# Score rows of the late groups: one partition from DRAM, spread by TensorE, copied by ScalarE

## The chip, the cores and the metric

The kernel runs on one core of one Trainium2 chip. The metric is device time in microseconds (us), the median of three runs. A profile of one further execution gives every instruction of the five engines (PE = TensorE, DVE = VectorE, ACT = ScalarE, POOL = GpSimd, SP = SyncE, which here only issues loads), and the DMA engines.

## What is computed

Two layers over 8192 nodes with 128 features; the adjacency matrix `adj` is 8192 x 8192, f32. Layer 0 multiplies `x` by the row-normalised matrix, and by a weight, then adds and normalises. Layer 1 is the part the change is in:

```
x_tangent = logmap0(x, C)
adj_att_par = adj   * sigmoid(s_left[:, None] + s_right[None, :] + b)      # w_par
adj_att_chi = adj.T * sigmoid(s_left[:, None] + s_right[None, :] + b)      # w_chi
support_t = adj_att_chi @ x_tangent + adj_att_par @ x_tangent
x = layernorm(x + proj(expmap0(support_t)))
```

`s_left` and `s_right` are vectors with one score per node. A sigmoid needs a sum of one score per row and one per column for every element of a matrix block.

## The kernel before

**Tiles and units.** Output columns are cut into 8 panels of 1024 nodes (`BP`), rows into 64 tiles of 128. A *unit* is one tile of 128 rows times one panel: 512 units in a fixed order (`plan`). For unit n ACT writes two sigmoids of 128x1024: `chi` into SBUF (L756) and `ps` into a PSUM slot (L773). Each has the panel's *score rows* as input and the tile's column scores as bias. POOL multiplies chi by the block of the matrix (L548), DVE multiplies ps by the transposed block (L1036) and adds both (L1045), and PE takes the sum into the panel's output in PSUM (L1244: two matmuls of 512 columns, each of which shows as two hardware instructions in the profile). Every eighth unit or so is *apart* (`APART`): DVE leaves the sum out, and PE takes both products (L1244 and L1250).

**Score rows.** `scores` has three buffers of [128, 2, 1024]: both rows of a panel (par and chi), the same in all 128 partitions. The rows themselves are written to DRAM (`plcl_d`, L709) as layer 0 finishes a panel. `load_rows` (L715) reads one row of 4 KB and broadcasts it to 128 partitions, 512 KB a load, two loads a panel, on ACT's DMA queue.

**Groups.** Units that stand in a row and belong to one panel are a *group*. Units 0 to 153 are spread between the steps of layer 0. From unit 154 on layer 1 runs alone (the late stage): a group of 64 units for each of the panels 3 to 7, and after each of the first three a group of 8 units that ends one of the panels 0 to 2. Groups thus start at 168, 232, 240, 304, 312, 376, 384 and 448. The eight groups whose rows are loaded anew take turns in score buffers 0 and 1. A buffer's next rows are loaded two units after the buffer's last user (`ROW_LOAD_AT`: units 153, 161, 233, 241, 305, 313, 377, 385), long before they are used.

**What sets the order.** Each engine's program is written out by hand, in a loop over n; semaphores join them. Between the units stand a finished panel's steps, at fixed offsets from a base (`FINALS`: 232, 266, 304, 338, 376, 410, 448, 512): ACT takes the output out of PSUM at +3 (`evacuate`, L796) and squares it at +4 (L807), PE sums the squares at +4 (L1269), ACT takes roots at +7. The output is one PSUM tile, so PE's first product of the next group waits for the evacuation (`out_evac`). For groups of 8 units `evacuate_early_panel` (L801) does the same, four units after the group's end (before unit 243).

**Buffers.** chi has four buffers late on: chi of unit n needs that of unit n - 4, which is free when the sum was made, or, for an apart unit, when PE has read it (`kt_used`). The PSUM slots for ps are two up to unit 194 and three after (`slot_plan`); a slot is free when its unit's sum (or apart product) is made. Loads of the matrix go through a ring of 10 to 11 entries of 1 MB, and SP issues a load as soon as its entry is free.

Of the kernel before, what the change touches and what calls it, by code (L numbers as in the profile page):

```python
# [151 lines left out]

def slot_plan():

    plans = {"unit": {}, "norms": {}, "final": {}}
    holder = {0: ("layer 0", 0), 1: ("passage", 0), 2: None}
    starts = {b + F_NORMS_SLOT: ("norms", k) for k, (_, b) in enumerate(FINALS)}
    starts |= {b + F_SLOT: ("final", k) for k, (_, b) in enumerate(FINALS)}
    uses = []
    for n in range(UNITS):  # L160
        if n in starts:
            uses.append(starts[n] + (n,))
        uses.append(("unit", n, n))
    uses += [("norms", len(FINALS) - 1, UNITS), ("final", len(FINALS) - 1, UNITS)]
    last = 2
    for kind, i, n in uses:
        if n < SLOT_TWO:
            s = 2
        elif n < SLOT_THREE:
            s = 0 if last == 2 else 2  # L170
        else:
            s = (last + 1) % SB
        last = s
        plans[kind][i] = (s, holder[s])
        holder[s] = (kind, i)
    return plans["unit"], plans["norms"], plans["final"]


SLOT_OF_UNIT, SLOT_OF_NORMS, SLOT_OF_FINAL = slot_plan()

# [85 lines left out]
ROW_LOAD_AT = {}  # L268
for _k, (_p, _t, _a) in enumerate(GROUPS):
    if _a == NPAN - 1:  # L270
        ROW_LOAD_AT.setdefault(ROWS_OF[_k][2] + 2, []).append(_k)

# [22 lines left out]
def adj_resnorm_kernel(nc, x_g, xT, g_blk, a_blk, WT, b_row, alpha, w_par, b_par, w_chi, b_chi, out):  # L297
    with ExitStack() as ctx:
# [21 lines left out]
        prcr = sb("prcr", [P, UPP * 2])  # L320
        ones = sb("ones", [P, 1])
        ident = sb("ident", [P, P])
        WTs = sb("WTs", [P, D])

        w4 = sb("w4", [P, 4])
# [62 lines left out]

        const_in = sem("const_in")
        ident_ready = sem("ident_ready")  # L390
        oma_ready = sem("oma_ready")
        bpc2_ready = sem("bpc2_ready")
        x_in = [sem(f"x_in{G}") for G in range(NG)]
# [28 lines left out]
        rowp_ready = sem("rowp_ready")  # L422
        rows_ready = sem("rows_ready")
        rows_out = sem("rows_out")

        c_ready = sem("c_ready")
        p_ready = sem("p_ready")
# [28 lines left out]
        def slot_free(eng, before):  # L456

            kind, i = before
            if kind == "unit" and i in APART:
                eng.wait_ge(m1_ready, i + 1)  # L460
            elif kind == "unit":
                eng.wait_ge(k_ready, SUMS[i])
            elif kind == "norms":
                eng.wait_ge(f_norm, i + 1)
            elif kind == "final":
                eng.wait_ge(v_ready, i + 1)
            elif kind == "layer 0":
                eng.wait_ge(y_evac, NPAN)
            else:
                eng.wait_ge(rows_ready, NPAN)  # L470
                eng.wait_ge(prcr_ready, NPAN)
# [58 lines left out]
        @block.gpsimd  # L530
        def _(pool):
            pool.memset(ones[:, :], 1.0).then_inc(ident_ready, 1)
            pool.memset(epsc[:, :], LN_EPS).then_inc(ident_ready, 1)
            pool.memset(ident[:, :], 0.0).then_inc(ident_ready, 1)
            pool.wait_ge(ident_ready, 3)
# [112 lines left out]
        def _(act):  # L648
# [63 lines left out]
            def load_rows(p, b):  # L712
                act.wait_ge(rows_out, 32 * (p + 1))
                for k in range(2):
                    act.dma_start(scores[:, b, k, :], plcl_d[k:k + 1, p * BP:(p + 1) * BP].to_broadcast([P, BP])) \  # L715
                        .then_inc(l_in[b], 16)

            def passage(r, tick):
                if tick == T_LOADX and r + 1 < NPAN:
                    load_xT(r + 1)  # L720
                if tick == T_SCALEX and r + 1 < NPAN:
                    scale_xT(r + 1)
                if tick == T_STD:
                    deviation(r)
                if tick == T_X1:
                    normalise(r)
                if tick == T_SQ:
                    squares(r)
                if tick == T_NRM:
                    norms(r)  # L730
                if tick == T_LN:
                    logarithm(r)
                if tick == T_XT:
                    tangent(r)
                if tick == T_XTT:
                    copy_turned_tangent(r)
                if tick == T_COPY:
                    copy_rows(r)
                if tick == T_LOADL and r < EARLY:
                    load_rows(r, r)  # L740


            def sigmoids(n):
                k, p, jt = UNIT[n]
                row, c, _ = rows_of(n)
                act.wait_ge(l_in[row], 32 * c)
                act.wait_ge(prcr_ready, jt // TPP + 1)
                b, before = buffer_of(n, CB)
                if before in APART:
                    act.wait_ge(kt_used, before + 1)  # L750
                elif before is not None:
                    act.wait_ge(k_ready, SUMS[before])
                elif b == CB:
                    act.wait_ge(l0_used, PAIRS)
                    act.wait_ge(res_ready, NPAN)
                act.activation(chi(n), scores[:, row, 1, :], ACT.Sigmoid,  # L756
                               bias=prcr[:, 2 * jt + 1:2 * jt + 2]).then_inc(c_ready, 1)
                if n in OWN_AT:
                    i = OWN_AT[n]
                    if i >= 2:  # L760
                        act.wait_ge(m1_ready, OWN[i - 2] + 1)
                    elif i == 1:
                        act.wait_ge(l0_used, PAIRS)
                        act.wait_ge(res_ready, NPAN)
                    else:
                        act.wait_ge(acc_added, ADDED_ALL)
                    dst = own_par[i % 2]
                else:
                    s, before = SLOT_OF_UNIT[n]
                    if before is not None:  # L770
                        slot_free(act, before)
                    dst = slots[s]
                act.activation(dst, scores[:, row, 0, :], ACT.Sigmoid,  # L773
                               bias=prcr[:, 2 * jt:2 * jt + 1]).then_inc(p_ready, 1)

            def next_rows(k):
                b, _, e = ROWS_OF[k]
                act.wait_ge(c_ready, e + 1)
                act.wait_ge(p_ready, e + 1)
                load_rows(GROUPS[k][0], b)  # L780

            def take_out(k):
                p, _, a = GROUPS[k]
# [104 lines left out]
            for n in range(N_EARLY, UNITS):  # L888
# [7 lines left out]
                    take_out(EVAC_AT_UNIT[n])  # L896
                if n - F_EVAC - 1 in LAST_OF_EARLY:
                    evacuate_early_panel(LAST_OF_EARLY[n - F_EVAC - 1])
                sigmoids(n)
            k = NPAN - 1  # L900
            act.preload_act_table(ACT.Sqrt)
# [256 lines left out]
        def _(pe):  # L1158
# [105 lines left out]
            def norms(k):  # L1264
# [4 lines left out]
                    ins = pe.matmul(slots[s][:, j:j + 1], columns(sqT, j), ones[:, 0:1], start=True, stop=True)  # L1269
                ins.then_inc(norms_ready, 1)  # L1270

            def turn(k):
                p, b = FINALS[k]
                pe.wait_ge(out_evac, GROUP_OF_FINAL[k] + 1)
# [20 lines left out]
            for n in range(N_EARLY, UNITS):  # L1295
                passage(NPAN - 1, LATE_PE.get(n - LATE0))
                for k, (_, b) in enumerate(FINALS):
                    if n == b + F_NORMS:
                        norms(k)
                    if n == b + F_TURN:  # L1300
                        turn(k)
                if n + 2 in OWN_AT:
                    turn_own(n + 2)
                products(n)
            norms(NPAN - 1)
            turn(NPAN - 1)
# [30 lines left out]
```

## Time and profile before

| | |
|---|---|
| median of 3 runs | 2198.63 us (2198.61 to 2199.72) |
| the profiled execution | 2200.13 us, span of its instructions 2198.3 us |
| busy, whole span | PE 2006.2, DVE 1929.8, POOL 1340.4, ACT 1318.0 us |
| DMA | 820.37 MB, mean 373 GB/s |
| score row loads | 22 of 512 KB, median 10.4 us from issue to landing |

A row of the timeline gives start, length, engine, line, operation, names and, in brackets, how long the engine stood idle before it and what ended that. Matmul ends are modelled; start to start is the safer reading. DMA share is the mean busy share of the 16 DMA engines. Times are from the first instruction of the profiled execution.

### The profile page before, as it was taken

How to read it: one execution, taken by the hardware profiler on the slowest of the kernel's cores; microseconds unless marked ns; L12 is line 12 of the kernel's file. 1: busy time of each engine (PE TensorE's matmuls, PEld its weight loads, DVE VectorE, ACT ScalarE, POOL GpSimd, SP SyncE). 2: the span in 40 equal slices, each digit the busy share in tenths (PEclk: the TensorE clock that was granted, in tenths of full speed). 3: DMA queues.
4: the chain of work that ended last, by engine and by line, in shares of the span. 5: the costliest groups of instructions: out<-in, count | busy, mean ns of one | idle time of the engine just before them, and what ended most of it. 6: DMA issues, size and time to landing. Idle time of an engine off the chain costs nothing. (4 is left out here: it accounts for less than half of the span.)

```text
span 2198.3 us, 18369 instructions
## 1 busy us (share of the span) xinstructions
PE 2006.2 (91%) x5072; PEld 898.4 (41%) x5072; DVE 1929.8 (88%) x1864; ACT 1318.0 (60%) x1508; POOL 1340.4 (61%) x639
## 2 busy tenths in 40 slices
PE   7999999999999998999999978898888888889886
PEld 3444444444444444444444433343333333334333
DVE  5757787988989989898999989999998998989896
ACT  0001324454464454454453588988989988989996
POOL 0000304534455554644544677999998998999996
PEclk9999999999999999999999988999999999999998
DMA  9978988989989989988989998999999999999993
GB/s 338 362 273 291 400 288 349 406 343 384 388 329 409 414 331 363 392 337 337 416 345 348 422 408 329 421 420 421 422 410 421 421 419 394 421 421 398 398 393 143
DMA packets 128453, 820.37 MB, mean 373 GB/s; under 512 B 14880, under 2 KB 27488, under 8 KB 31328
## 3 DMA queue, kind: packets, MB, share of 16 engines
q1 hardware_dynamic: 113392, 799.06, 90.7%
q10 hardware_dynamic: 14960, 20.13, 2.7%
q8 instruction: 42, 0.69, 0.1%
q14 instruction: 59, 0.48, 0.1%
HBM read 814.88 MB, written 4.26 MB: 373 GB/s over the span
## 5 line engine op out<-in xcount | busy, mean ns | idle before, releaser
L548 POOL TENSOR_TENSOR chi<-chi,ring 128x1024 f32<-128x1024 f32 x326 | 834.4, 2573 | 628.5 <-ACT chi L756 572.4
L1244 PE MATMUL ps<-keys,xtA 128*128 128x512 f32 x2048 | 981.3, 611 | 140.1 <-DVE keys L1045 110.5
L1171 PE MATMUL ps<-ring,xA 128*128 128x512 f32 x2048 | 918.4, 598 | 33.8 <-DMA xA<-in_x_g 15.2
L773 ACT ACTIVATE ps<-scores,prcr 128x1024 f32<-128x1024 f32 x492 | 544.2, 1106 | 394.2 <-DVE keys L1045 377.5
L1244 PEld LDWEIGHTS ps<-keys,xtA 128*128 128x128 f32 x2048 | 377.6, 193 | 683.8 <-issue 653.0
L935 DVE TENSOR_TENSOR dsum<-dsum,ring 128x2048 f32<-128x2048 f32 x240 | 594.1, 2475 | 30.4 <-DMA ring<-in_g_blk 24.4
L1171 PEld LDWEIGHTS ps<-ring,xA 128*128 128x128 f32 x2048 | 387.5, 192 | 519.1 <-issue 493.9
L1045 DVE TENSOR_TENSOR keys<-ps,chi 128x1024 f32<-128x1024 f32 x426 | 521.6, 1225 | 85.6 <-issue 31.3
L756 ACT ACTIVATE chi<-scores,prcr 128x1024 f32<-128x1024 f32 x426 | 483.8, 1136 | 16.3 <-DMA scores<-plcl_d 8.5
L1036 DVE TENSOR_TENSOR ps<-ps,ring 128x1024 f32<-128x1024 f32 x348 | 425.5, 1223 | 44.4 <-ACT ps L773 39.0
L548 POOL TENSOR_TENSOR chi<-chi,xA 128x1024 f32<-128x1024 f32 x79 | 185.7, 2366 | 18.4 <-ACT chi L756 18.4
L548 POOL TENSOR_TENSOR xA<-xA,ring 128x1024 f32<-128x1024 f32 x54 | 127.8, 2366 | 14.3 <-ACT xA L756 14.3
L756 ACT ACTIVATE xA<-scores,prcr 128x1024 f32<-128x1024 f32 x86 | 98.0, 1139 | 42.2 <-PE ps L1250 42.1
L1036 DVE TENSOR_TENSOR ps<-ps,xA 128x1024 f32<-128x1024 f32 x90 | 110.0, 1222 | 9.6 <-ACT ps L773 9.6
L541 POOL TENSOR_TENSOR dsum<-dsum 128x1024 f32<-128x1024 f32 x8 | 18.8, 2353 | 127.9 <-DVE dsum L935 125.4
L1250 PE MATMUL ps<-xA,xtA 128*128 128x512 f32 x148 | 70.5, 599 | 0.0
L1045 DVE TENSOR_TENSOR keys<-ps,xA 128x1024 f32<-128x1024 f32 x49 | 60.0, 1225 | 2.7 <-POOL xA L548 1.0
L548 POOL TENSOR_TENSOR xA<-xA 128x1024 f32<-128x1024 f32 x23 | 54.3, 2362 | 4.1 <-ACT xA L756 4.1
L756 ACT ACT_TABLE_LOAD x28 | 35.9, 1283 | 34.4 <-DVE prcr L1002 27.9
L557 POOL TENSOR_TENSOR acc<-taken,acc 128x1024 f32<-128x1024 f32 x15 | 37.3, 2487 | 31.0 <-ACT taken L789 31.0
L548 POOL TENSOR_TENSOR chi<-chi,scores 128x1024 f32<-128x1024 f32 x21 | 49.5, 2363 | 6.2 <-ACT chi L756 6.2
L661 ACT ACT_TABLE_LOAD x1 | 1.3, 1283 | 76.5 <-issue 76.5
(122 smaller groups left out, 820.9 us busy)
## 6 DMA issues: line engine op xcount, KB each, us to landing
ring<-in_g_blk SPq DMA_DIRECT2D x443, 1024.0 KB, 8.6
ring<-in_a_cols SPq DMA_DIRECT2D x190, 1024.0 KB, 10.0
xA<-in_a_cols SPq DMA_DIRECT2D x51, 1024.0 KB, 11.9
xA<-in_g_blk SPq DMA_DIRECT2D x44, 1024.0 KB, 10.0
scores<-in_a_cols SPq DMA_DIRECT2D x15, 1024.0 KB, 11.7
scores<-in_g_blk SPq DMA_DIRECT2D x15, 1024.0 KB, 10.7
scores<-plcl_d ACTq DMA_DIRECT2D x22, 512.0 KB, 10.4
xA<-in_x_g ACTq DMA_DIRECT2D x64, 64.0 KB, 11.8
```

The costliest lines, as they stand in the source:

```text
L541: pool.tensor_tensor(out=dsum[:, 0:BP], in0=dsum[:, 0:BP], in1=dsum[:, BP:2 * BP], op=ALU.add).then_inc(folded, 1)
L548: pool.tensor_tensor(out=chi(n), in0=chi(n), in1=half(t, n), op=ALU.mult).then_inc(m2_ready, 1)
L557: pool.tensor_tensor(out=at, in0=taken[:, :], in1=at, op=ALU.add).then_inc(acc_added, 1)
L661: act.activation(yb[:, :], yb[:, :], ACT.Copy, scale=oma[:, 0:1]).then_inc(xTs_scaled, 1)
L756: act.activation(chi(n), scores[:, row, 1, :], ACT.Sigmoid, bias=prcr[:, 2 * jt + 1:2 * jt + 2]).then_inc(c_ready, 1)
L773: act.activation(dst, scores[:, row, 0, :], ACT.Sigmoid, bias=prcr[:, 2 * jt:2 * jt + 1]).then_inc(p_ready, 1)
L935: dve.tensor_tensor(out=dsum[:, :], in0=dsum[:, :], in1=t, op=ALU.add).then_inc(deg_added, 1)
L1036: dve.tensor_tensor(out=keys(n) if n in APART else s, in0=s, in1=other, op=ALU.mult).then_inc(m1_ready, 1)
L1045: dve.tensor_tensor(out=keys(n), in0=slots[SLOT_OF_UNIT[n][0]], in1=chi(n), op=ALU.add).then_inc(k_ready, 1)
L1171: ins = pe.matmul(Y[:, h * BANK:(h + 1) * BANK], xA[:, tile * D:(tile + 1) * D], t[:, tt * BP + h * BANK:tt * BP + (h + 1) * BANK], start= ...
L1244: ins = pe.matmul(outp[:, h * BANK:(h + 1) * BANK], xtA[:, jt * D:(jt + 1) * D], keys(n)[:, h * BANK:(h + 1) * BANK], start=begins, stop=i ...
L1250: ins = pe.matmul(outp[:, h * BANK:(h + 1) * BANK], xtA[:, jt * D:(jt + 1) * D], chi(n)[:, h * BANK:(h + 1) * BANK], start=False, stop=is_ ...
```

## The change

For the eight late groups the load brings each row to one partition only: `scores[0:1, b, k, :]`, 4 KB. It is issued one unit earlier, one unit after the buffer's last user. PE then multiplies a row of ones [1, 128] with it (`send_rows`: two matmuls of 512 columns into a PSUM slot), which gives the row in all 128 partitions, and ACT copies it to `scores` (`copy_sent_rows`). `slot_plan` gives each row a turn in the rotation of the PSUM slots, as if it were a unit. The sends stand on PE before the products of the units `CAST_AT` - 2, the copies on ACT before the sigmoids of `CAST_AT` + 1; `CAST_AT` is 156, 157, 164, 165, 236, 237, 244, 245, 308, 309, 316, 317, 380, 381, 388 and 389. The three early panels keep their broadcasts. The core of the diff:

```
-        ROW_LOAD_AT.setdefault(ROWS_OF[_k][2] + 2, []).append(_k)
+        ROW_LOAD_AT.setdefault(ROWS_OF[_k][2] + 1, []).append(_k)
+ROW_CAST = 4
+CAST_LAG = 1
+CASTS = [(_k, _s) for _n in sorted(ROW_LOAD_AT) for _k in ROW_LOAD_AT[_n] for _s in range(2)]
+    _n = ROWS_OF[_k][2] + 1 + ROW_CAST + _s
...
+        if n in CAST_AT:
+            uses.append(("rows", CAST_AT[n], n))
         uses.append(("unit", n, n))
...
+            def load_late_rows(p, b):
+                act.wait_ge(rows_out, 32 * (p + 1))
+                for k in range(2):
+                    act.dma_start(scores[0:1, b, k, :], plcl_d[k:k + 1, p * BP:(p + 1) * BP]).then_inc(l_in[b], 16)
+            def copy_sent_rows(i):
+                k, which = CASTS[i]
+                act.wait_ge(rows_sent, i + 1)
+                act.activation(scores[:, ROWS_OF[k][0], which, :], slots[SLOT_OF_ROWS[i][0]], ACT.Copy).then_inc(rows_here, 1)
...
                 act.wait_ge(c_ready, e + 1)
                 act.wait_ge(p_ready, e + 1)
-                load_rows(GROUPS[k][0], b)
+                load_late_rows(GROUPS[k][0], b)
...
+                if n - CAST_LAG in CAST_AT:
+                    copy_sent_rows(CAST_AT[n - CAST_LAG])
                 sigmoids(n)
...
+            def send_rows(i):
+                pe.wait_ge(l_in[b], 32 * c)
+                s, before = SLOT_OF_ROWS[i]
+                slot_free(pe, before)
+                for h in range(BP // BANK):
+                    ins = pe.matmul(slots[s][:, at], ones_row[:, :], scores[0:1, b, which, at], start=True, stop=True)
+                ins.then_inc(rows_sent, 1)
...
+                if n + 2 in CAST_AT:
+                    send_rows(CAST_AT[n + 2])
                 products(n)
```

PE from the start of group 232, before (products of a unit are x2, an apart unit has L1250 too; L1236 loads the panel's earlier sum, L1269 sums the squares):

```order
L1236 MATMUL ps<-acc,ident 128x512 x2
L1244 MATMUL ps<-keys,xtA 128x512 x6
L1250 MATMUL ps<-xA,xtA 128x512 x2
L1244 MATMUL ps<-keys,xtA 128x512 x2
L1269 MATMUL ps<-ones,dsum 128x1 x8
L1244 MATMUL ps<-keys,xtA 128x512 x14
L1250 MATMUL ps<-xA,xtA 128x512 x2
```

The same place in the changed kernel (L1277, L1285, L1291 and L1310 are those lines, L1322 is the send):

```order
L1277 MATMUL ps<-acc,ident 128x512 x2
L1285 MATMUL ps<-keys,xtA 128x512 x4
L1322 MATMUL ps<-scores,ones_row 128x512 x2
L1285 MATMUL ps<-keys,xtA 128x512 x2
L1291 MATMUL ps<-xA,xtA 128x512 x2
L1322 MATMUL ps<-scores,ones_row 128x512 x2
L1285 MATMUL ps<-keys,xtA 128x512 x2
L1310 MATMUL ps<-ones,dsum 128x1 x8
L1285 MATMUL ps<-keys,xtA 128x512 x12
L1322 MATMUL ps<-scores,ones_row 128x512 x2
L1285 MATMUL ps<-keys,xtA 128x512 x2
L1291 MATMUL ps<-xA,xtA 128x512 x2
```

Two sends now stand around the apart unit 234 and the next two around the apart unit 242.

ACT at unit 235, before (L796 takes the panel out, L807 squares it):

```order
L796 ACTIVATE dsum<-ps 128x1024
L756 ACTIVATE chi<-scores,prcr 128x1024
L773 ACTIVATE ps<-scores,prcr 128x1024
L807 ACTIVATE dsum<-dsum 128x1024
L756 ACTIVATE chi<-scores,prcr 128x1024
L773 ACTIVATE ps<-scores,prcr 128x1024
L756 ACTIVATE chi<-scores,prcr 128x1024
L773 ACTIVATE ps<-scores,prcr 128x1024
L756 ACTIVATE xA<-scores,prcr 128x1024
```

The same place in the changed kernel (L835, L795, L812 and L846 are those lines, L752 is the copy):

```order
L835 ACTIVATE dsum<-ps 128x1024
L795 ACTIVATE chi<-scores,prcr 128x1024
L812 ACTIVATE ps<-scores,prcr 128x1024
L846 ACTIVATE dsum<-dsum 128x1024
L795 ACTIVATE chi<-scores,prcr 128x1024
L812 ACTIVATE ps<-scores,prcr 128x1024
L752 ACTIVATE scores<-ps 128x1024
L795 ACTIVATE chi<-scores,prcr 128x1024
L812 ACTIVATE ps<-scores,prcr 128x1024
L752 ACTIVATE scores<-ps 128x1024
L795 ACTIVATE xA<-scores,prcr 128x1024
```

A copy now stands ahead of the sigmoids of unit 237 and another ahead of those of unit 238 (the chi that goes to xA).

## Rows read from the trace of the kernel before

**Rows 1.** Windows: busy us PE, PEld, DVE, ACT, POOL; granted clock, DMA share, GB/s.

```profile
1400.00:1500.00 100.00, 89.25 (x233) 38.91 (x232) 91.53 (x79) 91.51 (x89) 95.53 (x47) 1.00 1.01 421
...
1859.00:1867.00 8.00, 7.49 (x14) 3.28 (x15) 6.63 (x7) 7.17 (x9) 7.75 (x9) 0.79 1.02 422
```

**Rows 2.** Waits, 1300 to 2180 us: who for whom, total us, times, longest.

```profile
ACT xA L756 <- PE ps L1250: 42.1, 27, 2.4
POOL chi L548 <- ACT chi L756: 38.7, 24, 6.3
...
POOL xA L548 <- ACT xA L756: 19.9, 17, 5.4
```

**Rows 3.** Waits of SP's load queue in the same stretch.

```profile
SPq L519 <- POOL chi L548: 609.3, 160, 8.0
```

**Rows 4.** Groups by line: busy us, mean ns of one, idle before.

```profile
L789 ACT ACTIVATE taken<-ps 128x1024 f32<-128x1024 f32 x15 | 15.2, 1013 | 17.3 <-PE ps L1244 17.2
```

**Rows 5.** The tile plcl_d: its DMAs, ns to issue min/median/max, us to landing.

```profile
L709 ACTq DMA_DIRECT2D plcl_d<-yb x16: 246/290/521, 213.8 to 1368.7; - x16
...
DMA to landing us min/median/max: 5.2/10.4/16.3
```

**Rows 6.** Timeline of PE from group 232 on.

```profile
1468.27 5.31 PE L1244 MATMUL ps<-keys,xtA 128*128 128x512 f32 x12
1473.42 1.88 PE L1250 MATMUL ps<-xA,xtA 128*128 128x512 f32 x4
1475.14 1.88 PE L1244 MATMUL ps<-keys,xtA 128*128 128x512 f32 x4
...
1489.76 5.42 PE L1244 MATMUL ps<-keys,xtA 128*128 128x512 f32 x12 [2.31 <-ACT acc L801]
1495.02 1.88 PE L1250 MATMUL ps<-xA,xtA 128*128 128x512 f32 x4
```

**Rows 7.** Timeline of ACT at the same place (evacuation, units 235, 237, 238; 243, 246).

```profile
1465.37 1.02 ACT L796 ACTIVATE dsum<-ps 128x1024 f32<-128x1024 f32 x1 [0.98 <-PE ps L1244]
1466.29 1.14 ACT L756 ACTIVATE chi<-scores,prcr 128x1024 f32<-128x1024 f32 x1
...
1471.40 1.14 ACT L756 ACTIVATE chi<-scores,prcr 128x1024 f32<-128x1024 f32 x1
...
1475.42 1.15 ACT L756 ACTIVATE xA<-scores,prcr 128x1024 f32<-128x1024 f32 x1 [1.88 <-PE ps L1250]
...
1488.70 1.00 ACT L801 ACTIVATE acc<-ps 128x1024 f32<-128x1024 f32 x1
...
1497.02 1.15 ACT L756 ACTIVATE xA<-scores,prcr 128x1024 f32<-128x1024 f32 x1 [1.01 <-PE ps L1250]
```

**Rows 8.** Timeline of POOL there: units 238, 239 and 246.

```profile
1476.71 2.35 POOL L548 TENSOR_TENSOR xA<-xA 128x1024 f32<-128x1024 f32 x1 [1.43 <-ACT xA L756]
1481.67 2.37 POOL L548 TENSOR_TENSOR chi<-chi,xA 128x1024 f32<-128x1024 f32 x1 [2.60 <-ACT chi L756]
...
1499.19 2.37 POOL L548 TENSOR_TENSOR xA<-xA,ring 128x1024 f32<-128x1024 f32 x1
```

**Rows 9.** Timeline of ACT at groups 304 and 376: units 310, 318, 382, 390.

```profile
1659.95 1.15 ACT L756 ACTIVATE xA<-scores,prcr 128x1024 f32<-128x1024 f32 x1 [1.88 <-PE ps L1250]
...
1681.64 1.15 ACT L756 ACTIVATE xA<-scores,prcr 128x1024 f32<-128x1024 f32 x1 [0.59 <-PE ps L1250]
...
1845.07 1.15 ACT L756 ACTIVATE xA<-scores,prcr 128x1024 f32<-128x1024 f32 x1 [1.88 <-PE ps L1250]
...
1868.46 1.15 ACT L756 ACTIVATE xA<-scores,prcr 128x1024 f32<-128x1024 f32 x1 [2.29 <-PE ps L1250]
```

**Rows 10.** Timeline of PE after the second evacuation at group 376.

```profile
1859.51 7.11 PE L1244 MATMUL ps<-keys,xtA 128*128 128x512 f32 x12 [2.31 <-ACT acc L801]
```

**Rows 11.** Timeline of DVE: the sum of unit 156, the product of unit 158.

```profile
1253.47 1.23 DVE L1045 TENSOR_TENSOR keys<-ps,chi 128x1024 f32<-128x1024 f32 x1 [2.27 <-POOL chi L548]
...
1257.01 1.22 DVE L1036 TENSOR_TENSOR ps<-ps,ring 128x1024 f32<-128x1024 f32 x1
```

More of the change, by code:

```diff
@@ L153, in slot_plan @@
 def slot_plan():
-    plans = {"unit": {}, "norms": {}, "final": {}}
+    plans = {"unit": {}, "norms": {}, "final": {}, "rows": {}}
     holder = {0: ("layer 0", 0), 1: ("passage", 0), 2: None}
@@ L175, in slot_plan @@
         holder[s] = (kind, i)
-    return plans["unit"], plans["norms"], plans["final"]
-SLOT_OF_UNIT, SLOT_OF_NORMS, SLOT_OF_FINAL = slot_plan()
+    return plans["unit"], plans["norms"], plans["final"], plans["rows"]
 ROWS_GONE = max(k for k, (p, _, a) in enumerate(GROUPS) if p == 2 and a < NPAN - 1)
@@ L270 @@
     if _a == NPAN - 1:
-        ROW_LOAD_AT.setdefault(ROWS_OF[_k][2] + 2, []).append(_k)
+        ROW_LOAD_AT.setdefault(ROWS_OF[_k][2] + 1, []).append(_k)
+ROW_CAST = 4
+CAST_LAG = 1
+CASTS = [(_k, _s) for _n in sorted(ROW_LOAD_AT) for _k in ROW_LOAD_AT[_n] for _s in range(2)]
+CAST_AT = {}
+for _i, (_k, _s) in enumerate(CASTS):
+    _n = ROWS_OF[_k][2] + 1 + ROW_CAST + _s
+    assert _n not in CAST_AT
+    CAST_AT[_n] = _i
+CAST_OF = {_k: 2 * _i + 2 for _i, (_k, _) in enumerate(CASTS[::2])}
+SLOT_OF_UNIT, SLOT_OF_NORMS, SLOT_OF_FINAL, SLOT_OF_ROWS = slot_plan()
 MORE = LATE0 + 16
@@ L322, in adj_resnorm_kernel @@
         ident = sb("ident", [P, P])
+        ones_row = sb("ones_row", [1, P])
         WTs = sb("WTs", [P, D])
@@ L390, in adj_resnorm_kernel @@
         ident_ready = sem("ident_ready")
+        ones_row_ready = sem("ones_row_ready")
         oma_ready = sem("oma_ready")
@@ L424, in adj_resnorm_kernel @@
         rows_out = sem("rows_out")
+        rows_sent = sem("rows_sent")
+        rows_here = sem("rows_here")
         c_ready = sem("c_ready")
@@ L466, in slot_free @@
                 eng.wait_ge(v_ready, i + 1)
+            elif kind == "rows":
+                eng.wait_ge(rows_here, i + 1)
             elif kind == "layer 0":
@@ L532, in _ @@
             pool.memset(ones[:, :], 1.0).then_inc(ident_ready, 1)
+            pool.memset(ones_row[:, :], 1.0).then_inc(ones_row_ready, 1)
             pool.memset(epsc[:, :], LN_EPS).then_inc(ident_ready, 1)
@@ L745, in sigmoids @@
                 row, c, _ = rows_of(n)
-                act.wait_ge(l_in[row], 32 * c)
+                if k in CAST_OF:
+                    act.wait_ge(rows_here, CAST_OF[k])
+                else:
+                    act.wait_ge(l_in[row], 32 * c)
                 act.wait_ge(prcr_ready, jt // TPP + 1)
@@ L1270, in norms @@
                 ins.then_inc(norms_ready, 1)
+            def send_rows(i):
+                k, which = CASTS[i]
+                b, c, _ = ROWS_OF[k]
+                pe.wait_ge(l_in[b], 32 * c)
+                pe.wait_ge(ones_row_ready, 1)
+                s, before = SLOT_OF_ROWS[i]
+                slot_free(pe, before)
+                for h in range(BP // BANK):
+                    at = slice(h * BANK, (h + 1) * BANK)
+                    ins = pe.matmul(slots[s][:, at], ones_row[:, :], scores[0:1, b, which, at], start=True, stop=True)
+                ins.then_inc(rows_sent, 1)
             def turn(k):
```

## The prediction

> **What bounds the kernel now.** The changed work lies in the late stage, from unit 154 on (about 1240 us to 2175 us). I read that stage in three steps. First the windows [rows 1]: in 100 us DVE is busy 91.53, ACT 91.51, POOL 95.53 and PE 89.25 us, and the DMA engines are full (share 1.01, 421 GB/s). Five resources are near their ends at once, so shares do not decide; the waits must. Second, who waits for whom between 1300 and 2180 us [rows 2]: POOL waits 38.7 + 19.9 = 58.6 us for ACT's sigmoids, ACT 42.1 us for PE's L1250, and no row of that answer names a DMA. SP instead waits 609.3 us in that stretch for POOL to free ring entries [rows 3]: data wait for compute, not compute for data. So compute sets the pace and the full DMA engines are a closed loop's queue.
>
> Third, the places where POOL stops. At a change of groups (first unit 232, then 304 and 376) ACT must take the finished panel out before PE may begin the next group. PE begins late and works off a backlog: after the evacuation at 1465.37 [rows 7] it runs 12, 4 and 4 instructions without a gap [rows 6]. ACT's chi for unit 238 needs the buffer of unit 234, an "apart" unit whose last reader is PE's L1250, and waits 1.88 us for it [rows 7]. POOL then stands 1.43 us before unit 238 and 2.60 us before unit 239 [rows 8]. Eight units later PE waits 2.31 us for the next evacuation [rows 6] and ACT waits 1.01 us before unit 246 [rows 7]. Near these places PE's backlog, then ACT, is the critical path. The change puts its new work exactly there, two units after each place's start.
>
> **What is removed.** 16 of the 22 broadcast loads of 512 KB go; 16 loads of one 4 KB row come. 16 x 524,288 B = 8.39 MB; at 421 GB/s [rows 1] that is 19.9 us of DMA time. I cost it at nothing gained, because no engine waits for a load in that stage [rows 2]; ring entries only land earlier and lie longer.
>
> The Trainium skill, "DMA: Bandwidth & Descriptors" (Specifications), puts the fabric's ceiling at 435 GB/s, so 421 would be 97% of what can be had and 19.3 us of it would come free. The trace agrees that the engines are full; by that rule alone the kernel would gain, and that is the second rival below.
>
> **What is added, on its own.** PE: 16 sends of two 128x512 f32 matmuls, four hardware instructions each. No row shows a matmul from one partition. The nearest is L1244 with the same 512 columns: 12 take 5.31 us, four take 1.72 (1473.42 to 1475.14 [rows 6]). Bounds: 0.43 us (if one partition cost as little as one of the four instructions) and 3.4 us (the same four at the halved clock, seen as 0.79 mean with 12 in 7.11 us [rows 1, 10]). I take 1.72, the row of equal shape. ACT: 16 copies PSUM to SBUF of 128x1024; L789 is that instruction, 1013 ns [rows 4], and 0.92 us start to start (1465.37 to 1466.29, [rows 7]). So 27.5 us of PE and 14.7 us of ACT in all; POOL's added memset lies before the first load and costs nothing visible.
>
> The Trainium skill, "TensorE: Matmul & The Clock Gate" (Step-by-step: what each phase is for), says a matmul's time goes by its columns and that "row count K doesn't matter here" for the weight load. By it a send from one partition costs as much as from 128, which is the value taken; no run here shows it yet.
>
> **What it does at a group change, worked at unit 232.** (1) The first pair of sends stands on PE before the products of units 234 and 235. Unit 234's L1250 therefore ends 1.72 us later, and the second send another 1.72 us after that. ACT's second copy stands before the sigmoids of unit 238, waits for the second send, and takes 0.92 us: chi 238 starts 1.72 + 1.72 + 0.92 = 4.4 us after its present 1475.42. The first copy disappears in the wait of 1.88 us that was there. Queued behind the waiting copy are all later sigmoids, since ACT runs in order; POOL was already idle for 1.43 and 2.60 us there [rows 8], so it cannot absorb it: +4.4 us on POOL. (2) The row load of the next group moves from unit 241 to 240 and now waits for the sigmoid that ACT has just started. The issue of two loads (0.29 us each by the small store of L709, [rows 5]) is no longer covered: c 240 starts about 0.7 us later, half of which POOL feels: +0.4 us. (3) The second pair stands before the products of units 242 and 243, again in a backlog that starts at an evacuation (1488.70, [rows 7]). chi 246 comes 4.4 us later for the same reason. POOL's product 246 started at 1499.19, while its input was ready at 1497.02 + 1.15 = 1498.17; less 0.15 us of signal, 0.9 us of that is slack: +3.5 us, and the ACT part of (2), 0.3 us, comes in here. Sum: 4.4 + 0.4 + 3.5 + 0.3 = 8.6 us. After that POOL and DVE run back to back again, so nothing is given back.
>
> At units 304 and 376 the same 1.88 us stand before the fourth-later chi, and 0.59 and 2.29 us in place of 1.01 [rows 9]. I take 8.6 us for each. In the last, PE had its clock halved for a moment (12 in 7.11 us, [rows 10]); if it is not halved there now, 1.7 us come back.
>
> **The first two late groups** (units 154 to 166) differ: only two PSUM slots turn over, and a row takes one of them for two units. Unit 157's sigmoid into PSUM must wait for unit 156's sum, which ends at 1253.47 + 1.23 = 1254.70 [rows 11]; then come that sigmoid, the copy (0.92) and unit 158's two sigmoids (at most 1.15 each, [rows 7]): DVE can take unit 158 at 1254.70 + 0.92 + 3 x 1.15 = 1259.1 at the latest, not 1257.01: +2.1 us, and 1.9 with the sigmoids' overlap of about 0.1. The second pair falls on DVE's residual work of the last passage, which covers it; I allow 0.6 us. Together 2.5 us, between 0 and 6.
>
> **Sum.** 3 x 8.6 + 2.5 = 28.3 us. The profiled execution took 2200.13 us (span 2198.3) and would take 2228.4; the median of the runs is 2198.63, 1.5 lower, so **2227 us**.
>
> **Rivals.** About 0.2% (4.4 us) is what a measurement of this kernel can tell from no change.
> (A) Only ACT's own time counts. If PE sends in gaps before its backlog, ACT pays 16 x 0.92 = 14.7 us and nothing waits: 2213. For: ACT runs 91% busy [rows 1]. Against: the order of PE puts the sends behind two products of the new group, and those behind the evacuation.
> (B) Faster: loads bind after all. Place: the ring in the late stage. If units followed landings, 19.9 us would go: 2198.6 - 19.9 = 2179. For: DMA share 1.01. Against: [rows 2, 3]. It decides from the point where POOL or DVE waits for a ring entry; here neither does.
> (C) Hidden: the copies fit into ACT's present waits (1.88 and 1.01 us, each over 0.92) and the sends into PE's 2.31 us: 2199 to 2203. Against: those waits exist because PE is late, and the sends make it later.
> (D) More: the small rows land late. A broadcast needs 5.2 to 16.3 us, median 10.4 [rows 5]; from the issue for the second pair to its first send I count about 11 us. If a 4 KB row behind a full ring takes 16, PE waits 5 us more at three places; or the clock halves during the sends. Either gives 10 to 15 us more: 2240.
>
> **Chances.** Forecast 0.50, (A) 0.20, (D) 0.13, (C) 0.10, (B) 0.07. Faster 0.07, within 0.2% 0.10, slower 0.83. The range takes in the forecast, (A) with the first groups' low bound and one-instruction sends (2207), and (D) with its upper end (2242).
>
> **What would show it.** Right: the sends' rows at 1.7 us for four; ACT rows of the copy with waits of 0.5 to 3 us released by PE; POOL's stops before units 238 and 239 grown by about 4.4 us together and a new stop before 246; DMA share below 1.0 in the late stage. Wrong: sends much shorter than 1.7 us; POOL's waits for ACT not above 58.6 us by some 25 us; any wait of PE for the rows' landing (then D); a load wait that vanished (then B).

## The result and the profile after

| | before | changed kernel |
|---|---|---|
| median of 4 runs each, same chip | 2198.62 us (2198.38 to 2199.72) | 2229.68 us (2227.95 to 2232.71) |
| the profiled execution | 2200.13 us, span 2198.3 us | 2227.95 us, span 2226.2 us |
| DMA, whole span | 820.37 MB | 812.04 MB |

The ratio is 1.0137, with a 95% interval of 1.0124 to 1.0150: the changed kernel is about 30 us slower. The forecast was 2227 us. The profiled execution was the fastest of the four, with a mean granted clock of TensorE of 0.984 (the slowest, 2232.71 us, had 0.979), so the traces show 27.8 of the 31 us between the medians; the rest lies in executions that have no trace.

**Where the time came from.** For each unit I subtract its start in the trace of before from its start in the trace of after; I take DVE's product (L1036 before, L1077 after) where nothing else is said. A number that stays the same over many units means that nothing is lost there. The difference is 0.99 us at unit 154, where the late stage begins. It grows at three places and is constant between them:

| place | before it | after it | grows by |
|---|---|---|---|
| units 154 to 194 (first two late groups) | 0.99 | 0.98 | 0.0 |
| units 236 to 250 (group 232) | 1.01 | 10.69 | 9.7 |
| units 303 to 350 (group 304) | 10.75 | 20.00 | 9.3 |
| units 375 to 430 (group 376) | 20.02 | 28.85 | 8.8 |
| units 430 to 510 | 28.85 | 28.80 | 0.0 |

Inside the first place: from unit 236 to 238 it grows from 1.01 to 5.90 (first pair of rows, 4.9), at unit 240 to 6.15 (row loads, 0.25), and from unit 244 to 250 from 6.31 to 10.69 (second pair, 4.4).

The timeline of PE after, at group 232 (start, length, engine, line, operation, names, shapes, count, and in brackets the idle time before and what ended it). L1322 is the send; this answers [rows 6]:

```profile
1467.51 1.98 PE L1277 MATMUL ps<-acc,ident 128*128 128x512 f32 x4 [1.11 <-ACT dsum L835]
1469.33 3.60 PE L1285 MATMUL ps<-keys,xtA 128*128 128x512 f32 x8
1472.85 1.98 PE L1322 MATMUL ps<-scores,ones_row 1*128 1x512 f32 x4
1474.76 1.98 PE L1285 MATMUL ps<-keys,xtA 128*128 128x512 f32 x4
1476.58 1.88 PE L1291 MATMUL ps<-xA,xtA 128*128 128x512 f32 x4
1478.39 1.98 PE L1322 MATMUL ps<-scores,ones_row 1*128 1x512 f32 x4
...
1496.47 3.70 PE L1285 MATMUL ps<-keys,xtA 128*128 128x512 f32 x8 [3.12 <-ACT acc L840]
1500.10 1.98 PE L1322 MATMUL ps<-scores,ones_row 1*128 1x512 f32 x4
```

The sends stand inside PE's backlog: from 1467.51 on PE has no gap. A send takes 1472.85 to 1474.76, that is 1.91 us, where the products of before took 1.72 [rows 6].

The timeline of ACT after, at the same place. L752 is the copy, L795 the chi sigmoid, L747 the load of two rows; this answers [rows 7]:

```profile
1466.43 1.02 ACT L835 ACTIVATE dsum<-ps 128x1024 f32<-128x1024 f32 x1 [0.99 <-PE ps L1285]
...
1474.87 1.03 ACT L752 ACTIVATE scores<-ps 128x1024 f32<-128x1024 f32 x1 [2.35 <-PE ps L1322]
1475.79 1.14 ACT L795 ACTIVATE chi<-scores,prcr 128x1024 f32<-128x1024 f32 x1
...
1480.41 1.03 ACT L752 ACTIVATE scores<-ps 128x1024 f32<-128x1024 f32 x1 [2.47 <-PE ps L1322]
1481.33 1.14 ACT L795 ACTIVATE xA<-scores,prcr 128x1024 f32<-128x1024 f32 x1
...
1488.51 0.53 ACTq L747 DMA_DIRECT2D scores<-plcl_d  x2
...
1502.11 1.03 ACT L752 ACTIVATE scores<-ps 128x1024 f32<-128x1024 f32 x1 [1.48 <-PE ps L1322]
...
1507.65 1.03 ACT L752 ACTIVATE scores<-ps 128x1024 f32<-128x1024 f32 x1 [2.47 <-PE ps L1322]
1508.58 1.14 ACT L795 ACTIVATE xA<-scores,prcr 128x1024 f32<-128x1024 f32 x1
```

Each copy waits 1.5 to 2.5 us for its send, and the sigmoid behind it starts 0.92 us after the copy does. The chi of unit 238 (1481.33) no longer waits for its apart buffer, as it did for 1.88 us before [rows 7]: the copy ahead of it waits longer.

The timeline of POOL after, units 237 to 239 and then 245 and 246; this answers [rows 8]:

```profile
1477.07 2.35 POOL L573 TENSOR_TENSOR chi<-chi,ring 128x1024 f32<-128x1024 f32 x1 [3.05 <-ACT chi L795]
1482.61 2.36 POOL L573 TENSOR_TENSOR xA<-xA 128x1024 f32<-128x1024 f32 x1 [3.19 <-ACT xA L795]
1487.57 2.36 POOL L573 TENSOR_TENSOR chi<-chi,xA 128x1024 f32<-128x1024 f32 x1 [2.60 <-ACT chi L795]
...
1504.32 2.35 POOL L573 TENSOR_TENSOR chi<-chi,ring 128x1024 f32<-128x1024 f32 x1 [1.11 <-ACT chi L795]
1509.85 2.37 POOL L573 TENSOR_TENSOR xA<-xA,ring 128x1024 f32<-128x1024 f32 x1 [3.19 <-ACT xA L795]
```

POOL stands 3.05 + 3.19 + 2.60 = 8.84 us before units 237 to 239, where it stood 1.43 + 2.60 = 4.03 us [rows 8]: 4.8 us more, the size of the first pair. Before units 245 and 246 it now stands 4.30 us. Who waits for whom after, from 1300 to 2208 us (total us, times, longest), to be held against [rows 2]:

```profile
POOL chi L573 <- ACT chi L795: 51.3, 33, 6.3
...
POOL xA L573 <- ACT xA L795: 33.0, 18, 5.4
ACT xA L795 <- PE ps L1291: 29.8, 19, 2.4
ACT scores L752 <- PE ps L1322: 25.5, 12, 2.5
```

POOL waits 84.3 us for ACT's sigmoids, 25.7 us more than before. ACT waits 25.5 us for sends, all of it in the twelve copies of the three places. No row names a DMA. Windows after (start and end, length, busy us of PE, PEld, DVE, ACT, POOL, then the granted clock, DMA share, GB/s):

```profile
1400.00:1500.00 100.00, 87.77 (x228) 37.49 (x226) 87.32 (x75) 88.67 (x87) 90.51 (x41) 1.00 0.98 404
```

Against [rows 1] the DMA share fell from 1.01 to 0.98, and POOL's busy time from 95.53 to 90.51 us: the same work is spread over more time.

### The profile page after: what moved, and what is told of

The parts are those of the page before. It is cut to its first block and busy times, and to the rows that moved or that the text cites. A ratio compares the mean times of both kernels' runs of the same rounds, so it can differ in the third digit from the quotient of the medians.

```text
span 2226.2 us, 18530 instructions
## 1 busy us (share of the span) xinstructions
PE 2031.4 (91%) x5136; PEld 903.2 (41%) x5136; DVE 1930.7 (87%) x1864; ACT 1332.9 (60%) x1524; POOL 1341.4 (60%) x640
## 2 busy tenths in 40 slices
DMA packets 126181, 812.04 MB, mean 365 GB/s; under 512 B 14640, under 2 KB 27248, under 8 KB 29056
## 5 line engine op out<-in xcount | busy, mean ns | idle before, releaser
L1285 PE MATMUL ps<-keys,xtA 128*128 128x512 f32 x2048 | 977.8, 608 | 142.9 <-DVE keys L1086 111.2
L812 ACT ACTIVATE ps<-scores,prcr 128x1024 f32<-128x1024 f32 x492 | 544.2, 1106 | 386.9 <-DVE keys L1086 369.4
L1285 PEld LDWEIGHTS ps<-keys,xtA 128*128 128x128 f32 x2048 | 373.5, 192 | 688.1 <-issue 654.1
L795 ACT ACTIVATE chi<-scores,prcr 128x1024 f32<-128x1024 f32 x426 | 484.0, 1136 | 20.8 <-DMA scores<-plcl_d 7.7
L1077 DVE TENSOR_TENSOR ps<-ps,ring 128x1024 f32<-128x1024 f32 x348 | 425.7, 1223 | 65.0 <-ACT ps L812 62.7
L1077 DVE TENSOR_TENSOR ps<-ps,xA 128x1024 f32<-128x1024 f32 x90 | 110.0, 1222 | 15.9 <-ACT ps L812 15.9
L795 ACT ACTIVATE xA<-scores,prcr 128x1024 f32<-128x1024 f32 x86 | 97.9, 1139 | 29.8 <-PE ps L1291 29.8
L566 POOL TENSOR_TENSOR dsum<-dsum 128x1024 f32<-128x1024 f32 x8 | 18.8, 2354 | 128.4 <-DVE dsum L976 126.0
L1291 PE MATMUL ps<-xA,xtA 128*128 128x512 f32 x148 | 69.5, 592 | 0.0
```

Source lines behind the costliest of these rows:

```text
L566: pool.tensor_tensor(out=dsum[:, 0:BP], in0=dsum[:, 0:BP], in1=dsum[:, BP:2 * BP], op=ALU.add).then_inc(folded, 1)
L795: act.activation(chi(n), scores[:, row, 1, :], ACT.Sigmoid, bias=prcr[:, 2 * jt + 1:2 * jt + 2]).then_inc(c_ready, 1)
L812: act.activation(dst, scores[:, row, 0, :], ACT.Sigmoid, bias=prcr[:, 2 * jt:2 * jt + 1]).then_inc(p_ready, 1)
L1077: dve.tensor_tensor(out=keys(n) if n in APART else s, in0=s, in1=other, op=ALU.mult).then_inc(m1_ready, 1)
L1285: ins = pe.matmul(outp[:, h * BANK:(h + 1) * BANK], xtA[:, jt * D:(jt + 1) * D], keys(n)[:, h * BANK:(h + 1) * BANK], start=begins, stop=i ...
L1291: ins = pe.matmul(outp[:, h * BANK:(h + 1) * BANK], xtA[:, jt * D:(jt + 1) * D], chi(n)[:, h * BANK:(h + 1) * BANK], start=False, stop=is_ ...
```

## The experiments

The times of the kernel before that go with each ratio were taken on the same chip as the experiment: medians 2200.22 us (the first four experiments) and 2198.85 us (the last three).

**Rows only.** Do the loads bind? This takes the kernel before and makes the late loads small, without sends or copies: 127 partitions keep the scores that stood there, here as in the copies and the sends alone below.

```
-                load_rows(GROUPS[k][0], b)
+                load_late_rows(GROUPS[k][0], b)
```

> The kernel before, with the late groups' rows loaded to one partition only, nothing sent and nothing copied: the spreading over partitions is left out, so the late sigmoids use old rows. This is the removed DMA work alone, 8.39 MB less. Theory (no engine waits for a load in the late stage, compute sets the pace): within 0.2% of before, 2196 to 2202 us; DMA share in the late windows falls from 1.01 to about 0.98 and nothing else moves. Rival (loads bind, 19.9 us of DMA time come free): about 2179 us.

Measured: 2198.45 us, ratio 0.9994 (0.9985 to 1.0002). In its trace, which was longer in layer 0, the difference to before is 6.2 us at unit 154 and 7.0 us at unit 510, without a place where it falls. So 8.39 MB less at a share of 1.01 buys nothing: the loads bind nothing, and the rival with 2179 us falls. The expected share of about 0.98 came in two of the five windows of 100 us from 1400 to 1900 us only (0.98 and 0.97, against 1.01 and 0.99 before); the other three stayed at 1.01.

**Second pairs later.** Is the second pair dear because it stands in the backlog behind an evacuation? Its sends and copies are moved 18 units on (42 for the first group), where PE has gaps.

```
+LATER = {19: 42, 21: 18, 23: 18, 25: 18}
...
-    _n = ROWS_OF[_k][2] + 1 + ROW_CAST + _s
+    _n = ROWS_OF[_k][2] + 1 + ROW_CAST + LATER.get(_k, 0) + _s
```

> The changed kernel with the second pair of each place (rows of the groups of 8 units' successors in buffer 1) sent and copied 18 units later (42 for the first), away from PE's backlog after an evacuation; the first pairs stay. Theory (a pair costs because it stands in the backlog): the second pairs' 4.5 us at three places go, 13.5 us, and about 1.5 us come back where they now stand: 2216 us, 2213 to 2220. Rival (a pair costs its own ACT and PE time wherever it stands): no change, 2229 us.

Measured: 2229.03 us, ratio 1.0131 (1.0117 to 1.0144). My expectation missed, and the moved pairs cost where they stand now: 3.1 us from unit 206 to 212, 3.7 us from unit 262 to 273, 3.4 us at each of the two others. At the three old places 1.0, 0.8 and 0.4 us stayed too: there the granted clock of PE fell, and twelve instructions took 6.9 to 7.0 us (a row, and a table, stand at the end of this document). The time is the rival's, 2229 us; that its reason does not hold is shown by two of the next experiments, copies only and copies three units after. The timeline of ACT in this kernel at a moved pair (L753 is the copy):

```profile
1545.67 1.15 ACT L796 ACTIVATE xA<-scores,prcr 128x1024 f32<-128x1024 f32 x1 [2.43 <-PE ps L1292]
...
1549.22 1.02 ACT L753 ACTIVATE scores<-ps 128x1024 f32<-128x1024 f32 x1 [1.20 <-PE ps L1323]
...
1553.04 1.03 ACT L753 ACTIVATE scores<-ps 128x1024 f32<-128x1024 f32 x1 [0.75 <-PE ps L1323]
```

and of PE there (L1323 is the send, L1292 the second product of an apart unit):

```profile
1540.17 3.67 PE L1286 MATMUL ps<-keys,xtA 128*128 128x512 f32 x8 [0.64 <-DVE keys L1087]
1543.67 1.88 PE L1292 MATMUL ps<-xA,xtA 128*128 128x512 f32 x4
1545.39 1.88 PE L1286 MATMUL ps<-keys,xtA 128*128 128x512 f32 x4
1547.20 1.98 PE L1323 MATMUL ps<-scores,ones_row 1*128 1x512 f32 x4
```

The copies wait here as well, with no evacuation near. The order says why: with its slot's turn at unit c, a row is sent ahead of PE's products of unit c - 2, which PE reaches only when DVE's sums are made, and copied ahead of ACT's sigmoids of unit c + 1. ACT runs so far ahead of PE that it comes to the copy first, and the sigmoids are queued behind it. The new theory is therefore: such a pair costs wherever the copy comes to ACT's turn before the send is done, backlog or not.

**Copies only.** The rows are loaded small, nothing is sent, and ACT copies the row buffer onto itself when the row has landed.

```
-                act.wait_ge(rows_sent, i + 1)
-                act.activation(scores[:, ROWS_OF[k][0], which, :], slots[SLOT_OF_ROWS[i][0]], ACT.Copy).then_inc(rows_here, 1)
+                act.wait_ge(l_in[b], 32 * c)
+                act.activation(scores[:, b, which, :], scores[:, b, which, :], ACT.Copy).then_inc(rows_here, 1)
```

> The changed kernel without the sends and their PSUM slots: ACT copies each row buffer onto itself in SBUF at the same places, waiting for the row's landing only. The spreading over partitions is left out, so late sigmoids use old rows. Theory (copies of 0.92 us fit in waits of ACT for PE that are there anyway; the cost is the wait for the sends): 2198 to 2203 us. Rival (ACT's own time counts, 16 x 0.92 us): 2213 us.

Measured: 2204.22 us, ratio 1.0016 (1.0005 to 1.0028), 3.5 us more, a little above what I expected and far from the rival's 2213. The timeline of ACT (L751 is the copy, the last row the chi of unit 238):

```profile
1469.07 1.04 ACT L751 ACTIVATE scores<-scores 128x1024 f32<-128x1024 f32 x1
...
1472.09 1.05 ACT L751 ACTIVATE scores<-scores 128x1024 f32<-128x1024 f32 x1
1473.09 1.15 ACT L794 ACTIVATE xA<-scores,prcr 128x1024 f32<-128x1024 f32 x1
```

and of PE behind the second evacuation there:

```profile
1488.23 7.11 PE L1284 MATMUL ps<-keys,xtA 128*128 128x512 f32 x12 [3.12 <-ACT acc L839]
```

The first pair's copies fill the 1.88 us for which ACT stood before, and the difference to before is the same at units 236 and 239 (-2.3 us). Around the second pair 1.4 us are lost (-2.1 us at unit 240, -0.7 at 250), but not by the copies: behind both of them ACT still waits 0.77 us for PE, which is late, and 1.76 and 1.73 us at the other two places. PE waits 3.12 us for the evacuation in place of 2.31 (every kernel that loads the next rows one unit earlier has this evacuation 0.8 us later, and none that does not), and its twelve instructions then take 7.11 us in place of 5.42, in part at the lower clock; at groups 304 and 376 they take 8.48 and 8.45 (before: 5.42 and 7.11). ACT's own time is therefore covered. The one trace has 7.3 us more in the late stage, with 3.2 us less in layer 0, so the size is only known as between 3.5 and 7 us; the 6.4 us of it that are lost at the three places are not the copies' time.

**Sends only.** PE sends, nothing is copied, and a slot is free again as soon as its send is done.

```
-                eng.wait_ge(rows_here, i + 1)
+                eng.wait_ge(rows_sent, i + 1)
...
-                if n - CAST_LAG in CAST_AT:
-                    copy_sent_rows(CAST_AT[n - CAST_LAG])
```

> The changed kernel without the copies: PE sends each row to its PSUM slot at the same place, the slot is then free, and ACT reads nothing from it. The spreading to SBUF is left out, so late sigmoids use old rows. Theory: the sends lengthen PE's backlog; at each of three places the first pair costs the 4.2 us that PE is later when ACT waits for the sums of squares, the load 0.3, the second pair 1.5 after slack, 6.0 in all, and 1 to 2 in the first groups: 2218 us, 2212 to 2223. Rival (only ACT's copies and their time count): 2199 to 2203 us. Rival (the whole cost is PE's): 2229 us.

Measured: 2218.80 us, ratio 1.0083 (1.0069 to 1.0096), as expected. In its trace the late stage grows by 17.8 us: 7.8 at group 232, 5.8 and 5.4 at the other two, and 1.3 us less in the first groups, where 1 to 2 us more were expected. At group 232 the lower clock fell behind the evacuation (eight instructions in 5.20 us; 3.70 at the other two), which is most of what that place has above the others. The timeline of ACT there (L792 is chi, L809 the sigmoid into the slot):

```profile
1472.03 1.12 ACT L809 ACTIVATE ps<-scores,prcr 128x1024 f32<-128x1024 f32 x1 [1.28 <-PE ps L1317]
...
1475.74 1.15 ACT L792 ACTIVATE xA<-scores,prcr 128x1024 f32<-128x1024 f32 x1 [2.59 <-PE ps L1286]
...
1477.57 1.12 ACT L809 ACTIVATE ps<-scores,prcr 128x1024 f32<-128x1024 f32 x1 [0.68 <-PE ps L1317]
```

Without any copy the sends still make ACT wait: for the apart product that they push back (2.59 us in place of 1.88) and for the slots that they hold (1.28 and 0.68 us). By ratios, sends cost 18.3 us, copies 3.5, and both together 30.1; by the traces' late stages 17.8, 7.3 and 27.8. The two can't be added, as what copies only lost at the three places was not the copies' time. Place by place the traces say more. The first pair costs 4.2 us by its sends alone (units 236 to 239, and the same at the other two places) and 4.8 to 4.9 with its copies. The second pair costs 1.4 and 1.0 us by its sends alone at groups 304 and 376, where the clock stayed up, and 4.2 and 3.7 with its copies. So the first pair's price is mostly the sends in PE's backlog, and the second pair's mostly the copies' wait.

**Sends from 128 partitions.** The send took 1.91 us and not 1.72. Is it because the matmul has one row? Here the weights have 128 rows, of which all but the first are zero, and the moving tile has 128 partitions.

```
-        ones_row = sb("ones_row", [1, P])
+        ones_row = sb("ones_row", [P, P])
...
-                    ins = pe.matmul(slots[s][:, at], ones_row[:, :], scores[0:1, b, which, at], start=True, stop=True)
+                    ins = pe.matmul(slots[s][:, at], ones_row[:, :], scores[:, b, which, at], start=True, stop=True)
```

> The changed kernel with each send made from all 128 partitions of the row buffer, by weights that are one in row 0 and zero elsewhere, in place of a send from one partition; everything else is the same. In the changed kernel a send and the products beside it took 1.91 and 1.82 us where 1.72 was counted. Theory 1 (the weight load of a one-row matmul, and of the product after it, is not hidden behind the running matmul): a send takes 1.72 us again, about 0.8 us less for each pair at three places, 2224 to 2226 us. Theory 2 (a send costs this from any number of rows): 2229 us, rows unchanged.

Measured: 2230.54 us, ratio 1.0144 (1.0124 to 1.0163): no gain. By the time alone the theory of the single row falls. The rows say otherwise. The timeline of PE in this kernel at group 232 (L1324 is the send):

```profile
1472.19 1.88 PE L1324 MATMUL ps<-scores,ones_row 128*128 128x512 f32 x4
1473.91 1.88 PE L1287 MATMUL ps<-keys,xtA 128*128 128x512 f32 x4
...
1495.33 5.40 PE L1287 MATMUL ps<-keys,xtA 128*128 128x512 f32 x8 [3.14 <-ACT acc L842]
1500.56 1.88 PE L1324 MATMUL ps<-scores,ones_row 128*128 128x512 f32 x4
```

A send now takes 1.72 us start to start, and the first pair costs 4.3 us (units 236 to 238) in place of 4.9. But the eight instructions behind the second evacuation take 5.40 us in place of 3.70, and so again at groups 304 (5.40) and 376 (5.25): 5 us in all, more than the 3.6 us that the six pairs of the three places gain at 0.6 us each. The window of 10 us there, in this kernel and then in the changed kernel (columns as above):

```profile
1495.00:1505.00 10.00, 9.68 (x19) 4.27 (x20) 6.44 (x6) 7.02 (x9) 7.08 (x8) 0.83 1.00 385
```

```profile
1495.00:1505.00 10.00, 8.53 (x19) 3.54 (x20) 7.55 (x7) 8.52 (x10) 8.60 (x9) 1.00 0.99 397
```

A granted clock of 0.83 means that for about a third of these 10 us PE had the lower of its two levels (1.2 and not 2.4 GHz); in the changed kernel it had the higher one throughout. PE had stood for 3.14 us just before, but 3.12 us in the changed kernel, where the clock stayed up; over the 15 us from 1480 on it was busy for 9.92 us here and 11.27 us there. Which of these decides is left open. At groups 304 and 376 the changed kernel had the lower level too, but a few us earlier, under four instructions that stand ahead of the evacuation; at group 376:

```profile
1880.10 3.50 PE L1285 MATMUL ps<-keys,xtA 128*128 128x512 f32 x4 [2.17 <-DVE keys L1086]
1885.17 3.70 PE L1285 MATMUL ps<-keys,xtA 128*128 128x512 f32 x8 [1.58 <-ACT acc L840]
```

They took 3.50 us in place of 1.96, and the wait behind them was that much shorter, so nothing was lost. The single row does cost what I thought; in this trace its gain went into the clock. That a faster PE makes the clock fall is not shown.

**Copies three units after.** The second pairs of the late groups are moved 10 units on, the two rows of a pair stand four units apart, and the copy stands three units after the slot's turn, so that the send is long done. The plan of the slots passes over a slot that is held.

```
+            while busy.get(s, -1) > n:
+                s = (s + 1) % SB
...
+LATER = {19: 42, 21: 10, 23: 10, 25: 10}
+    _n = ROWS_OF[_k][2] + 1 + ROW_CAST + LATER.get(_k, 0) + (4 if _k in LATER else 1) * _s
+    LAG_OF[_i] = 3 if _k in LATER else 1
+COPY_AT = {_n + LAG_OF[_i]: _i for _n, _i in CAST_AT.items()}
```

> The changed kernel with the first pairs as they are; the second pairs stand 10 units later (42 for the first), 4 units apart, each copy 3 units after its slot's turn instead of 1, the other slots turning meanwhile. Moving the second pairs alone had changed nothing: there a pair still cost 3.1 to 3.7 us, with ACT standing 0.75 to 1.5 us before each copy. Theory (what a pair costs is ACT's wait, in order, for a send that PE has behind its products): with three units between, no copy waits, a second pair costs under 1 us, four places: 2229 - 12 = 2217 us, 2214 to 2220. Rival (a pair costs the time of the sends and copies themselves): 2226 to 2230 us.

Measured: 2219.75 us, ratio 1.0097 (1.0077 to 1.0116), as expected. In the trace a second pair costs 0.6 to 0.7 us at each of its four places, where it cost 3.1 to 3.7 us with the copy one unit after the turn. The first pair still costs 4.85 us. The send and its copy in this kernel, first from PE's timeline and then from ACT's (L1329 and L759):

```profile
1530.96 1.95 PE L1292 MATMUL ps<-keys,xtA 128*128 128x512 f32 x4 [0.64 <-DVE keys L1093]
1532.85 1.98 PE L1329 MATMUL ps<-scores,ones_row 1*128 1x512 f32 x4
```

```profile
1539.17 1.00 ACT L759 ACTIVATE scores<-ps 128x1024 f32<-128x1024 f32 x1
1540.08 1.13 ACT L802 ACTIVATE chi<-scores,prcr 128x1024 f32<-128x1024 f32 x1
```

The copy has no bracket: the send ended more than 4 us earlier, and ACT takes 0.91 us for the copy and nothing more. This is the new theory's main proof, and the rival of 2226 us and more falls: the same sends and copies stand there and cost 0.7 us. The place (10 units later and not 18), the wider spacing and the later copy were changed together, and which of them does more was not tried.

**Second pairs alone.** As the last one, but the first pairs are broadcast by DMA as before. What is left of the cost if the pair in the evacuation's backlog is gone?

```
-                load_late_rows(GROUPS[k][0], b)
+                (load_late_rows if k % 2 else load_rows)(GROUPS[k][0], b)
```

> As the last, and the first pairs (groups of 64 whose rows are needed 8 units after their buffer is free) are broadcast from DRAM as in the kernel before, two units after the buffer's last user. Half of the removed DMA work stays removed. Theory (loads bind nothing, lagged copies cost under 1 us a pair): 2199 to 2203 us, no gain on before. Rival (half of 19.9 us of DMA time comes back): 2189 us. Rival (the pairs cost their own ACT and PE time): about 2213 us.

Measured: 2200.99 us, ratio 1.0007 (0.9998 to 1.0016), as expected. With its sends and copies away from the evacuations the change costs no more than a measurement can tell (its trace has 3.1 us more in the late stage), and gains nothing either. The step to the experiment before, 2219.75 - 2200.99 = 18.8 us, is the price of the first pairs with their place: 4.85 us at each of three group changes, and the rest mostly eight units later, where that kernel still lost 1.1, 2.2 and 0.6 us without any send or copy there. Behind the evacuation its twelve instructions took 6.80, 8.33 and 7.11 us, against 5.42, 5.42 and 7.11 before: a part of that price is again the clock. No variant beat the kernel before.

## Why the prediction was right, point by point

**What bounds.** Right: compute sets the pace, the full DMA engines do not. The run with small rows alone shows it (0.9994). The Trainium skill, "DMA: Bandwidth & Descriptors" (Specifications), gives a fabric ceiling of 435 GB/s, and 421 GB/s at a share of 1.01 [rows 1] agrees that the engines were near it; a resource at its ceiling was still not what the time hung on.

**The first pair (4.4 us).** Right in its place and kind, short in size: 4.9 us. The send is 1.91 us and not 1.72, and the product between two sends takes 1.82 us (1474.76 to 1476.58), so 0.4 to 0.5 us were missing in the sum. One detail was wrong: I let the first copy vanish in the wait of 1.88 us. It has a wait of its own (2.35 us), and POOL's new stop therefore lies before units 237 and 238, not 238 and 239. The total of the stops, 4.8 us more, is the forecast 4.4 with the longer sends. By themselves, without any copy, the sends cost 4.2 us there.

**The row load (0.4 + 0.3 us).** 0.25 us on DVE at unit 240, 0.8 us on ACT's chi there. About right.

**The second pair (3.5 us).** Between unit 244 and the end of the place it costs 4.4, 4.2 and 3.7 us. Right in kind: with the 0.3 us of the row load that come in here 3.8 us were forecast, and the longer sends are about the rest (4.4 and 4.2 at the first two places). The reason, though, was too narrow: "again in a backlog that starts at an evacuation". The runs show that the same pair costs 3.1 to 3.7 us where there is no evacuation, and 0.6 to 0.7 us with the copies later and its two rows wider apart. What costs in this pair is mostly a copy that stands in ACT's order ahead of its own input (its sends alone cost 1.0 to 1.4 us); the backlog is one way to be late. The prediction's phrase "Queued behind the waiting copy are all later sigmoids" was the heart of it. For the first pair the backlog itself is most of the price.

**The group changes.** 3 x 8.6 = 25.8 us were forecast, 9.7 + 9.3 + 8.8 = 27.8 us came. At group 376 eight product instructions behind the evacuation took 3.70 us, without the lower clock of [rows 10], as the prediction allowed; that place is the cheapest, but by 0.5 and 0.9 us and not by the 1.7 us allowed. The lower level was not gone: it stood ahead of the evacuation.

**The first two late groups (2.5 us).** This term failed. DVE's product of unit 158 does come 1.9 us later (0.99 to 2.90), as worked out, but at unit 159 it is only 0.4 us later, and the second pair's 0.4 us (1.41 at unit 166, 1.85 at 168) is gone at unit 183: DVE stood 0.54 and 0.26 us for ACT and POOL there before the change, and does not after it. The step taken for granted was that a delay there stays. Copies of these groups wait for no send, and the delays lie in work that has room. So the sum (28.3 us forecast, 27.8 in the trace from unit 154 to 510) is right by two errors of 2 and 2.5 us that cancel: its closeness is luck, its kind and its three places are not.

**The rivals.** (A), ACT's own time at 2213, falls with the copies alone (2204.22, and behind the second copies ACT still waits for PE). (B) falls with the rows alone. (C), hidden, falls for this order, but the last experiment reaches its time with half of the pairs; an order that hides all eight was not tried. (D) did not occur: no send waits for a row's landing, and none ran at the lower clock.

## What to carry to other kernels

Moving work from a DMA queue to engines pays only where something waits for the DMA; look for that wait, not at the share of busy time. In an engine that runs its instructions in order, a small instruction costs as much as it waits: put a copy behind its producer by enough of the consumer's own work (here three units and not one, with the two rows wider apart, took a pair from 3.1 to 3.7 us down to 0.6 to 0.7), and keep producer and copy out of the stretch in which the producer works off a backlog. Where two steps are predicted with sums of small terms, trace the difference of start times along the units: it shows each term by itself, and which errors cancelled. Before a loss of a few us is put down to the change, look at the granted clock there.

## What the runs showed of the hardware

Between products from 128 partitions, a send from one partition is not cheaper than one from 128 but 0.19 us dearer: 1.91 against 1.72 us. The timeline of weight loads (PEld) shows why, first in the changed kernel, then with sends from 128 partitions:

```profile
1471.90 0.19 PEld L1285 LDWEIGHTS ps<-keys,xtA 128*128 128x128 f32 x1 [0.24 <-issue]
1472.85 0.29 PEld L1322 LDWEIGHTS ps<-scores,ones_row 1*128 1x128 f32 x2 [0.76 <-issue]
...
1474.76 0.30 PEld L1285 LDWEIGHTS ps<-keys,xtA 128*128 128x128 f32 x2 [0.76 <-issue]
```

```profile
1471.34 0.19 PEld L1287 LDWEIGHTS ps<-keys,xtA 128*128 128x128 f32 x1 [0.24 <-issue]
1471.76 0.19 PEld L1324 LDWEIGHTS ps<-scores,ones_row 128*128 128x128 f32 x1 [0.24 <-issue]
```

With one row the load starts at 1472.85, the very start of the send, and the next product's load likewise at its own start (1474.76). With 128 rows it starts at 1471.76, 0.43 us ahead of its send at 1472.19, under the matmul before it. So in these traces the load is not hidden at a change between one row and 128. The Trainium skill, "TensorE: Matmul & The Clock Gate" (Step-by-step: what each phase is for), says that row count doesn't matter for the time of a weight load: its duration agrees (0.18 to 0.19 us in both), but where the load stands does depend on it here.

The second surprise is the clock. Where the lower level falls near an evacuation decides over 1.5 to 3 us of PE's time, and it falls in another place from kernel to kernel. The kernel with later second pairs shows a mean of 0.66 over the 10 us from 1490:

```profile
1490.00:1500.00 10.00, 5.46 (x8) 2.18 (x9) 8.48 (x9) 10.00 (x11) 9.58 (x6) 0.66 0.83 328
```

How long the first product instructions behind the second evacuation took, in us, shows it for each trace (twelve take 5.42 and eight 3.70 where the clock stayed up):

| kernel | instructions | group 232 | group 304 | group 376 |
|---|---|---|---|---|
| before | 12 | 5.42 | 5.42 | 7.11 |
| rows only | 12 | 5.42 | 5.42 | 7.11 |
| changed kernel | 8 | 3.70 | 3.70 | 3.70 |
| second pairs later | 12 | 6.95 | 6.89 | 6.93 |
| copies only | 12 | 7.11 | 8.48 | 8.45 |
| sends only | 8 | 5.20 | 3.70 | 3.70 |
| sends from 128 partitions | 8 | 5.40 | 5.40 | 5.25 |
| copies three units after | 12 | 6.80 | 8.33 | 7.11 |
| second pairs alone | 12 | 5.42 | 7.11 | 5.42 |

The wait just before does not settle it: before the change it was 2.31 us at all three places, with 5.42, 5.42 and 7.11 us behind it. In the ten executions of copies only the fastest (2196.67 us) had a mean clock of 0.982 and the slowest (2208.90) 0.975. What makes the level fall is left open.
